# GpSimd keeps a running sum of the state products in SBUF, TensorE sums only the pairs that run alone

## What is computed

```python
# layer 0, feed-forward part: 8 experts, dense, top 2 weighted
h = jnp.einsum('te,ieh->tih', xf, w1) + b1
h = jax.nn.gelu(h)
out = jnp.einsum('tih,ihe->tie', h, w2) + b2
out = jnp.sum(out * weights[..., None], axis=1)
...
# layer 1, attention part: 16 states, 256 inner channels
def step(h, inp):
    dt_t, xv_t, B_t, C_t = inp
    dA = jnp.exp(dt_t[:, :, None] * A[None])
    h = dA * h + (dt_t * xv_t)[:, :, None] * B_t[:, None, :]
    y_t = jnp.einsum('bdn,bn->bd', h, C_t)
    return (h, y_t)
...
y = y * _silu(z)
return y @ W_out.T
```

## Time and profile before

| | us |
|---|---|
| three runs before | 669.57, 672.67, 674.6 (median 672.67) |
| profiled execution, its own time | 669.75 |
| its span | 667.7 |
| TensorE busy | 515.8 (77%) |
| VectorE busy | 431.0 (65%) |
| ScalarE busy | 369.2 (55%) |
| GpSimd busy | 355.1 (53%) |

### The profile page before, as it was taken

The page is one execution under the profiler, slowest core; times in us unless marked ns, Lnnn a source line. Parts: engine busy times, 40 slices in busy tenths (PEclk is TensorE's granted clock), DMA queues, the critical chain, the costliest instruction groups (busy, mean ns, idle before and its releaser), DMA issues.

```text
span 667.7 us, 6946 instructions
## 1 busy us (share of the span) xinstructions
PE 515.8 (77%) x2368; PEld 354.4 (53%) x2368; DVE 431.0 (65%) x727; ACT 369.2 (55%) x510; POOL 355.1 (53%) x224
## 2 busy tenths in 40 slices
PE   4578587559589889998878798788888768756673
PEld 4365455335477778676646557456557533333322
DVE  5658878832532333128886687696587698889972
ACT  1434142134454464769887888687788446745301
POOL 3127785633501011205878774978774857548551
PEclk9989897879789899999989999799899779978996
DMA  8500000000000000300101100112100111101100
GB/s 319 193 1 0 0 1 1 1 0 0 1 0 1 1 1 0 129 1 32 64 32 65 32 32 33 63 48 64 34 33 32 58 52 65 64 32 63 47 1 16
DMA packets 12562, 26.93 MB, mean 40 GB/s; under 512 B 1968, under 2 KB 7472, under 8 KB 12272
## 3 DMA queue, kind: packets, MB, share of 16 engines
q1 hardware_dynamic: 11952, 25.57, 10.9%
q10 hardware_dynamic: 576, 0.92, 0.4%
HBM read 25.31 MB, written 1.18 MB: 40 GB/s over the span
## 4 chain that ended last, share of the span: by engine, by line
PE 41%; DVE 27%; ACT 15%; issue 8%; POOL 7%; DMA 1%; ACTq 0%; POOLq 0%; DVEq 0%
PE pO L1183 9%; DVE Hs L724 8%; DVE pCT L711 5%; PE pH L1221 4%; ACT gel L934 4%; DVE S L619 4%; PE pH L1171 3%; PE pY L1265 3%; ACT dA L946 3%; PE pY L1258 3%; ACT L946 2%; DVE pH L618 2%; PE pH L1173 2%; POOL Zod L364 2%; POOL ZS L377 2%
## 5 line engine op out<-in xcount | busy, mean ns | idle before, releaser
L1183 PEld LDWEIGHTS pO<-w_e,gel 128*128 128x128 f32 x1024 | 129.3, 202 | 11.4 <-issue 9.8
L1183 PE MATMUL pO<-w_e,gel 128*128 128x128 f32 x1024 | 130.2, 285 | 0.0
L724 DVE TENSOR_TENSOR_SCAN Hs<-dA,HL,pCT 128x512 f32<-128x512 f32 x96 | 117.7, 1268 | 9.1 <-issue 4.0
L934 ACT ACTIVATE gel<-pH,b_e 128x512 f32<-128x512 f32 x128 | 86.4, 687 | 64.6 <-PE pH L1173 63.8
L711 DVE TENSOR_TENSOR pCT<-u,pB 128x1024 f32<-128x1024 f32 x64 | 78.4, 1225 | 41.7 <-PE pB L1246 40.7
L364 POOL TENSOR_TENSOR Zev<-Hs,Crow 128x1024 f32<-128x1024 f32 x32 | 75.6, 2363 | 54.8 <-DVE Hs L724 54.5
L946 ACT ACTIVATE dA<-dt,a_neg 128x512 f32<-128x512 f32 x128 | 81.8, 710 | 26.7 <-DVE Hs L724 26.5
L1171 PE MATMUL pH<-h2h,w_e1h 128*128 128x512 f32 x128 | 57.8, 452 | 19.2 <-ACT gel L934 17.6
L695 DVE SCALAR_TENSOR_TENSOR X<-pO,wts,X 128x128 f32<-128x128 f32 x128 | 35.9, 343 | 50.9 <-PE pO L1183 50.9
L364 POOL TENSOR_TENSOR Zod<-Hs,Crow 128x1024 f32<-128x1024 f32 x18 | 42.5, 2363 | 40.3 <-DVE Hs L724 40.3
L425 POOL TENSOR_TENSOR ZA<-Qsb,S 128x1024 f32<-128x1024 f32 x16 | 37.9, 2372 | 35.7 <-DVE S L619 32.8
(11 more groups left out here) (196 smaller groups left out, 974.9 us busy)
## 6 DMA issues: line engine op xcount, KB each, us to landing
Crow<-c_rows SPq DMA_DIRECT2D x32, 512.0 KB, 3.7
w_e<-in_w_e SPq DMA_DIRECT2D x2, 2048.0 KB, 10.7
X<-in_x SPq DMA_DIRECT2D x4, 256.0 KB, 6.8
out<-h2T SPq DMA_DIRECT2D x4, 256.0 KB, 2.2
S<-in_w_mod ACTq DMA_DIRECT2D x2, 384.0 KB, 4.6
w_cx<-in_conv_row SPq DMA_DIRECT2D x1, 512.0 KB, 9.5
w_f<-in_w_f SPq DMA_DIRECT2D x2, 128.0 KB, 5.8
b_e<-in_b_e SPq DMA_DIRECT2D x1, 256.0 KB, 13.3
```

Of the source, the lines that this page charges most:

```text
L724: vec.tensor_tensor_scan(Hs[:, 2 * o + d, 0:w], dA[:, 4 * (p % 2) + 2 * o + d, 0:w], pU[:, d, 0:w], HL[:, d, n:n + 1] if c else 0.0, ALU.m ...
L934: nc.scalar.activation(gel[:, n % NG, 0:w], pH[n % 2][:, 0:w], ACT.Gelu_apprx_tanh, bias=b_e1[:, NK * e + k:NK * e + k + 1]).then_inc(s["m ...
L1183: ins = mm(pO[:, j * P:(j + 1) * P], gel[:, n % NG, j * P:(j + 1) * P], w_e2[:, NK * (g % E) + k, :], start=(k == 0 and j == 0), stop=(k = ...
```

## The change

GpSimd now keeps one running sum a chunk, in one half of Zev (`acc_of(c)`, the halves alternate with the chunks). The chunk's first product is written there; each later product of a pair p < ALONE goes to Zod and is added in place at once, between the two products of the pair (L390 of the changed kernel). ZS is used for the pairs that run alone only. TensorE has no totals for p < ALONE. In slot 19, `total(ALONE)` first adds the running sum of chunk 2 (pairs 16 and 17) into pY, with two matmuls (L1269), and then pair 18's products as before. The gates of chunks 0 and 1, whose pairs all run beside experts (`summed`), read the running sum from SBUF instead of PSUM, and wait for GpSimd's last add of the chunk. The product of pair 19, whose place in Zev is the running sum's, waits for TensorE's total of slot 19.

```diff
         def totals(p):
-            return (p + 2) // 2 if not alone(p) else ALONE // 2 + p + 1 - ALONE
+            return p + 1 - ALONE
+        def summed(c):
+            return NP * (c + 1) <= ALONE
+        def adds(m):
+            return m - m // NS
+        def acc_of(c):
+            h = ND * ((c + 1) % 2)
+            return Zev[:, h:h + ND, 0:WIDTHS[c]]
...
             def output(p, o):
                 m, w = 2 * p + o, WIDTHS[p // NP]
+                c, k = divmod(p, NP)
                 h = slice(2 * (p % 2), 2 * (p % 2) + 2)
-                if o == 0:
-                    Z = Zev[:, h, 0:w]
-                    if p >= 2:
-                        pool.wait_ge(s["mam_y" if alone(p - 2) else "mam_zs"], totals(p - 2) if alone(p - 2) else p - 1)
-                elif alone(p):
-                    Z = ZS[:, h, 0:w]
-                    pool.wait_ge(s["mam_y"], totals(p - 2))
+                first = k == 0 and o == 0
+                if alone(p):
+                    Z = [Zev, ZS][o][:, h, 0:w]
+                    if p >= ALONE + 2:
+                        pool.wait_ge(s["mam_y"], totals(p - 2))
+                    elif o == 0 and p % 2 == (c + 1) % 2:
+                        pool.wait_ge(s["mam_y"], 1)
+                    elif o == 0:
+                        pool.wait_ge(s["mam_y2"], 2 * c)
+                elif first:
+                    Z = acc_of(c)
+                    if c >= 2:
+                        pool.wait_ge(s["mam_y2"], 2 * (c - 1))
                 else:
                     Z = Zod[:, :, 0:w]
-                    if p:
-                        pool.wait_ge(s["mam_zs"], p)
+                    if adds(m - 1):
+                        pool.wait_ge(s["mam_zs"], adds(m - 1))
...
-            def pair(p):
-
-                h, w = slice(2 * (p % 2), 2 * (p % 2) + 2), WIDTHS[p // NP]
-                pool.wait_ge(s["mam_z"], 2 * p + 2)
-                if p >= 2 and p % 2 == 0:
-                    pool.wait_ge(s["mam_y"], p // 2)
-                elif p >= 2:
-                    pool.wait_ge(s["mam_zq"], p // 2)
-                pool.tensor_tensor(ZS[:, h, 0:w], Zev[:, h, 0:w], Zod[:, :, 0:w], ALU.add).then_inc(s["mam_zs"], 1)
-                done["mam_zs"] = p + 1
-                if p % 2:
-                    pool.wait_ge(s["mam_zs"], p + 1)
-                    pool.tensor_tensor(ZS[:, 0:ND, 0:w], ZS[:, 0:ND, 0:w], ZS[:, ND:2 * ND, 0:w],
-                                       ALU.add).then_inc(s["mam_zq"], 1)
-                    done["mam_zq"] = p // 2 + 1
+                if not alone(p) and not first:
+                    pool.wait_ge(s["mam_z"], m + 1)
+                    pool.tensor_tensor(acc_of(c), acc_of(c), Z, ALU.add).then_inc(s["mam_zs"], 1)
+                    done["mam_zs"] = adds(m)
...
             def gate(c):
-                vec.wait_ge(s["mam_y"], totals(NP * (c + 1) - 1))
+                if summed(c):
+                    vec.wait_ge(s["mam_zs"], adds(NS * (c + 1) - 1))
+                else:
+                    vec.wait_ge(s["mam_y"], totals(NP * (c + 1) - 1))
                 for d in range(ND):
-                    vec.tensor_tensor(y2[:, d, 0:WIDTHS[c]], pY[d][:, 0:WIDTHS[c]], half_of(gz, c)[:, d, :], ALU.mult).then_inc(s["mam_y2"], 1)
+                    y = acc_of(c)[:, d, :] if summed(c) else pY[d][:, 0:WIDTHS[c]]
+                    vec.tensor_tensor(y2[:, d, 0:WIDTHS[c]], y, half_of(gz, c)[:, d, :], ALU.mult).then_inc(s["mam_y2"], 1)
...
             def total(p, b=None):
 
+                if not alone(p):
+                    return
                 c, k = divmod(p, NP)
-                if k <= 1 and c:
+                if k == 0 and c:
                     pe.wait_ge(s["mam_y2"], 2 * c)
                 h, w = 2 * (p % 2), WIDTHS[c]
-                if alone(p):
-                    for o, Z in ((0, Zev), (1, ZS)):
-                        pe.wait_ge(s["mam_z"], 2 * p + o + 1)
-                        for d in range(ND):
-                            ins = mm(pY[d][:, 0:w], ident[:, :], Z[:, h + d, 0:w], start=(k == 0 and o == 0),
-                                     stop=(k == NP - 1 and o == 1))
-                else:
-                    if p % 2 == 0:
-                        return
-                    pe.wait_ge(s["mam_zq"], p // 2 + 1)
+                if p == ALONE and k:
+                    pe.wait_ge(s["mam_zs"], adds(2 * p - 1))
                     for d in range(ND):
-                        ins = mm(pY[d][:, 0:w], ident[:, :], ZS[:, d, 0:w], start=(k == 1), stop=(k == NP - 1))
+                        mm(pY[d][:, 0:w], ident[:, :], acc_of(c)[:, d, :], start=True, stop=False)
+                for o, Z in ((0, Zev), (1, ZS)):
+                    pe.wait_ge(s["mam_z"], 2 * p + o + 1)
+                    for d in range(ND):
+                        ins = mm(pY[d][:, 0:w], ident[:, :], Z[:, h + d, 0:w], start=(k == 0 and o == 0),
+                                 stop=(k == NP - 1 and o == 1))
                 ins.then_inc(s["mam_y"], 1)
```

More of the change, by code:

```diff
@@ L225, in build @@
             mam_hist mam_xp mam_zp mam_gz mam_dtp mam_bc mam_bcs mam_xc mam_dt mam_u
-            mam_st0 mam_st mam_cd mam_bB mam_ub mam_dA mam_sc mam_z mam_zs mam_zq mam_y mam_y2 mam_o mam_x
+            mam_st0 mam_st mam_cd mam_bB mam_ub mam_dA mam_sc mam_z mam_zs  mam_y mam_y2 mam_o mam_x
             fft_o fft_b fft_x vec_chain act_chain pool_chain out_done""".split()
@@ L342, in gn @@
                 pool.tensor_tensor(gn_rs[:, :], gn_ve[:, :], mhalf[:, 0:1], ALU.pow).then_inc(s["gn_r"], 1)
-            done = {"mam_z": 0, "mam_zs": 0, "mam_zq": 0}
+            done = {"mam_z": 0, "mam_zs": 0}
             def output(p, o):
                 m, w = 2 * p + o, WIDTHS[p // NP]
+                c, k = divmod(p, NP)
                 h = slice(2 * (p % 2), 2 * (p % 2) + 2)
-                if o == 0:
-                    Z = Zev[:, h, 0:w]
-                    if p >= 2:
-                        pool.wait_ge(s["mam_y" if alone(p - 2) else "mam_zs"], totals(p - 2) if alone(p - 2) else p - 1)
-                elif alone(p):
-                    Z = ZS[:, h, 0:w]
-                    pool.wait_ge(s["mam_y"], totals(p - 2))
+                first = k == 0 and o == 0
[11 more added lines that the diff above has]
+                        pool.wait_ge(s["mam_y2"], 2 * (c - 1))
                 else:
                     Z = Zod[:, :, 0:w]
-                    if p:
-                        pool.wait_ge(s["mam_zs"], p)
+                    if adds(m - 1):
+                        pool.wait_ge(s["mam_zs"], adds(m - 1))
                 if o == 0:
@@ L473, in _ @@
                     output(p, 1)
-                    if not alone(p):
-                        pair(p)
                 for at, stage, c, *k in stages:
```

## The result

The change makes the kernel faster: 653.25 us in the median of 4 runs (650.72 to 657.37) against 672.58 (669.57 to 674.6), a ratio of 0.9722 with a 95% interval of 0.9682 to 0.9763. Timed again later the ratio was 0.9724. The profiled execution took 651.67 us, with 649.6 of span.

A forecast was written before the change was run, and what follows sets the result against it. A loop of waits through GpSimd's second add, TensorE's total and VectorE's row of B was taken as the bound. Slot gains of 20.9 us and the ledger's 17 gave 19, so 652 us; range 644 to 663.

The forecast's parts named there:

- The loop and the sum by slots: TensorE's queue: totals waiting for GpSimd's second add delay VectorE's row of B; gains in six slots sum to 20.9 us.
- Slot 12, where I expected GpSimd to be late: GpSimd, tightest in slots 10 and 11 (11.8 us each), delays slot 12's scans that reuse Hs; TensorE's gain there counted nothing.
- GpSimd's ledger: GpSimd's expert stretch: 209.4 us against 226.5, 184.5 busy; 29.4 us of adds free in waits before second products.
- Any wait for GpSimd costs: TensorE ahead of its down products: a late total costs its wait and slower matmuls after; such waits were 24.7 us.
- The rule on two SBUF inputs: Gates of chunks 0 and 1 reading SBUF: each may cost GpSimd 0.86 us once, under 2 us in all.
- New waits: GpSimd's in-place sums, pair 19's product, two gates: pair 19's wait for TensorE's total hidden, otherwise 1 to 2 us once.
- the slower rival: GpSimd's instructions stretch to 3.22 us beside VectorE: 24 us slower, 694 to 697 us; chance 0.05.
- ScalarE's gelu: Ahead of TensorE's up products in every slot, a wrong sign; rival with GpSimd or ScalarE as bound: 661 to 663, chance 0.15.

## Why the prediction was right

The forecast was 652 us and the measured median is 653.25; a gain of 19 us was forecast, and 19.3 measured.

*The loop and the sum by slots.* Right, and it is the step on which the number rests. VectorE's products behind a total came earlier, against its first product of the stretch, by 2.84 us in slot 2 (329.28 - 299.13 before, 328.35 - 301.04 now; forecast 2.75), and by 19.7 us behind slot 18 (forecast 20.9). In between every term of the sum came in, each read as the step by which VectorE's next product moved: 2.84, 4.5, 1.70, 4.93, 1.72 and 5.58 us in slots 2, 4, 6, 10, 14 and 18, forecast 2.75, 4.43, 1.7, 4.85, 1.7 and 5.49 (slot 10: 430.55 became 418.85, with no wait left). They make 21.3 us; the stretch gained 19.7, since 1.6 were lost elsewhere, 1.1 of it at the gate of chunk 1, which reads two inputs from SBUF (below). Another 2.0, at chunk 1's u product and the gate of chunk 0, was made up by slot 10. The prediction had taken 20.9 down to 19 for another reason, a late GpSimd and the lower sum of its ledger. So the mechanism was right, while the closeness of 19 to 19.3 owes something to luck.

*Slot 12, where I expected GpSimd to be late.* Right: the 1.3 us of wait for slot 12's row of B go, but the scans behind it (the first state of slot 13) wait 2.18 us for GpSimd's product, and at slot 14's first product the gain is 13.6 us, what it was at slot 12's:

```profile
438.54 1.22 DVE L717 TENSOR_TENSOR pCT<-u,pB 128x1024 f32<-128x1024 f32 x1
441.94 2.45 DVE L730 TENSOR_TENSOR_SCAN Hs<-dA,HL,pCT 128x512 f32<-128x512 f32 x2 [2.18 <-POOL Zod L384]
```

*GpSimd's ledger.* Its sum was good, 209.4 us for the stretch against 210.0, and 184.5 us of busy time against 186.0, but its reasoning was only partly right. I held the adds to be free because they fill the wait before the second product (29 us). The kernel with the adds behind both products lost 3 to 5 us, not 29: where GpSimd falls behind the wait closes by itself, in 6 of the 12 pairs that had it. What these two kernels suggest is that GpSimd's busy time against VectorE's pace matters more than where a single add lies.

*"Any wait for GpSimd costs."* I had treated the wait as the cause and the running sum as its removal. The wait put back alone cost 3 us of the 19 by the ratios, and 5.0 of 19.7 in the loop stretch. The last add of a pair is also done sooner, and the prediction had no term for that.

*The rule on two SBUF inputs.* One half of the term was right and the other missing. I charged GpSimd 0.9 us a gate and VectorE nothing. Measured: at each gate GpSimd lost 0.5 us in its product and 0.3 in its add, 0.85 together, and VectorE 2.2, of which 1.1 delayed its next product. That VectorE's u product, which the change leaves as it was, would take longer too (3.00 us for 1.23 in chunk 1) was not in the prediction. The Trainium skill (SBUF — State Buffer, Who interferes with whom) says that the second to issue blocks until the first is finished, and the trace agrees, within some 0.1 us, once the starts are read at the u product of chunk 1:

```profile
383.56 3.00 DVE L710 TENSOR_TENSOR u<-dt,xc 128x1024 f32<-128x1024 f32 x1 [2.15 <-ACT xc L911]
...
383.12 2.36 POOL L390 TENSOR_TENSOR Zev<-Zev,Zod 128x1024 f32<-128x1024 f32 x1
385.55 3.27 POOL L384 TENSOR_TENSOR Zod<-Hs,Crow 128x1024 f32<-128x1024 f32 x1
```

GpSimd's add ran from 383.12 to 385.48, VectorE's product came at 383.56 and ended at 386.56, 1.1 us after that add; GpSimd's next product came at 385.55 and ended 1 us late. So VectorE paid 1.8 us and GpSimd 0.9. In the earlier trace rows VectorE began at 390.30, 0.15 us before GpSimd's product of that time ended, and only GpSimd's next instruction paid:

```profile
388.10 2.35 POOL L364 TENSOR_TENSOR Zod<-Hs,Crow 128x1024 f32<-128x1024 f32 x1 [2.43 <-DVE Hs L724]
```

A GpSimd that runs without gaps has nearly always an instruction under way when VectorE's comes; I took the price from a row in which that instruction was all but done.

*New waits.* The wait of pair 19's product for the total is there and hidden, as forecast: GpSimd waited 3.40 us, and VectorE's scans of pair 20 (525.68) followed VectorE's own work without a gap.

```profile
521.80 2.34 POOL L384 TENSOR_TENSOR Zev<-Hs,Crow 128x1024 f32<-128x1024 f32 x1 [3.40 <-PE pY L1273]
...
524.42 1.22 DVE L717 TENSOR_TENSOR pCT<-u,pB 128x1024 f32<-128x1024 f32 x1
525.68 2.45 DVE L730 TENSOR_TENSOR_SCAN Hs<-dA,HL,pCT 128x512 f32<-128x512 f32 x2
```

*Rivals.* GpSimd's instructions did not stretch but beside VectorE's two-SBUF ones (means 2.45 and 2.39 us), so the slower rival had its mechanism right and its reach far too wide. ScalarE's gelu now ends the most idle time on TensorE (24.5 us in 17 waits), but it was 22.6 us in 17 waits before, so it has not become the bound.

## What to carry to other kernels

Read an in-order queue for what stands behind a wait, not for the wait: a sum that nobody needs soon held the row of B for which the busiest loop waited, and moving it some instructions down the queue gave some nine tenths of what a new way of summing gave (in the loop stretch, all of it). When a kernel's time varies by more than the effect, compare a stretch between two instructions of one engine in the traces. Before removing work, try the same work at a later place in the queue. When an engine is made to run without gaps, ask which instructions of its neighbour collide with it (here VectorE's with two SBUF inputs), and charge the neighbour as well, since it will mostly be the one that comes second.

## What was not expected of the hardware

VectorE's two gate instructions of 128 x 512 with both inputs in SBUF took 3.48 us beside a busy GpSimd and 1.28 us with one input in PSUM. The first took its own 0.68 us; meanwhile a product of GpSimd had started (395.43), and the second did not end until 0.5 us behind it (398.87 against 398.33). So one short VectorE instruction can take four times its own length (the longest took 2.88):

```profile
L743 DVE TENSOR_TENSOR y<-Zev,gz x4: 680/1772/2881, 395.4 to 489.5; 128x512 f32<-128x512 f32 x4
L743 DVE TENSOR_TENSOR y<-pY,gz x4: 678/686/692, 569.8 to 633.3; 128x512 f32<-128x512 f32 x4
```

And a TensorE idle for 1.9 us kept a granted clock of 1.00 here (412 to 417 us), while the 4.38 us of the earlier trace rows were followed by 0.50; in the kernel with wait and matmuls back, 1.84 us of idling stood before two matmuls of 3.35 us, with a granted clock of 0.58 (517.2 to 520.6 us). So the idle time ahead does not by itself tell what clock follows; what else decides it was not tried.
